# A perceiver block on one core: the first step's orders laid anew, and the gate's logits taken from transposed unnormalised tokens

## The chip, the core and the metric

One core of a Trainium2 chip runs the whole program. The metric is the device time in microseconds of one execution; lower is better. The core has five engines with queues of their own, each worked off in order: TensorE (PE; its weight loads are shown as PEld), VectorE (DVE), ScalarE (ACT), GpSimd (POOL) and SyncE (SP), which issues most DMA transfers. They wait for one another with semaphores only.

## What is computed

Three residual layers on 32 batches of 32 tokens of 512 channels, that is T = 1024 tokens: cross-attention to 257 context rows per batch with 16 heads, a mixing layer in the frequency domain, and a mixture of 8 experts of which each token takes the one with the largest gate logit.

```python
x = x + xattn(layernorm(x), ctx, ctx, mask)     # Q = ln(x) Wq.T + bq; softmax; weights @ V; @ Wo.T + bo
x = x + mix(layernorm(x))                       # sum over tokens of bind(k, v), unbound by each q (FFT)
l = layernorm(x)                                # (x - mean) / sqrt(var + eps)
logits = l @ Wg + bg                            # 512 x 8
one_hot = one_hot(argmax(logits), 8)
x = x + sum_e one_hot[:, e] * (gelu(l @ W1[e]) @ W2[e])
```

## The kernel before

Tokens lie in NT = 8 tiles of 128; HT = 4 of them are a half. KC = 4 chunks of 128 channels. Products are made in float16 with each operand split in a high half (`hi`, ScalarE, a rounded copy) and a low half (`lo`, VectorE, what the rounding left), so that one product is three passes: high x high, high x low, low x high (`hl_passes`). A layer norm takes `bn_stats` and `bn_aggr` on VectorE, the power −0.5 on GpSimd (`power`), and the normalisation `(x − mean) * rstd` on VectorE (`normalise`). `LN_GROUPS` lists the tiles of each norm: groups 0 and 1 are the halves for the cross-attention, 2 and 3 those for the mixing, 4 (tiles 0 to 3), 5 (4, 5) and 6 (6, 7) those for the experts.

The cross-attention runs in STEPS = 16 steps of two batches. Step 0 is laid out by hand (`first_step` on ScalarE and VectorE, a straight list on TensorE and GpSimd), steps 1 to 15 are a loop. In step 0 TensorE makes the keys of the first context (`first_keys`), its values (`first_values`), transposes of the normalised tokens in fp32 (`transpose_tokens`), eight query products (`queries`, one per half of the tokens and chunk), the keys and values of the 257th context row (the two products that count `last_ps`), and the scores of both batches. ScalarE moves each result out (`query`, `tokens_hi`), GpSimd rounds queries (`query_hi`), VectorE takes the low halves (`query_lo`, `tokens_lo`). SyncE stores the last row's values to DRAM and loads them again re-laid (semaphore `vlast_stored`); VectorE's `scores` may only write after that store, since both use the same memory. GpSimd spreads the queries over the heads (`queries_of`, counts `q_ready`). After the softmax the probabilities' high and low halves are transposed by DMA (`p_transposed`: one transfer per batch, once `p_lo` is done), and the attention of step 0 stands behind the keys of step 1 on TensorE.

The third layer norm and the gate overlap the end of the mixing layer. `spectra` are 24 products of 512 columns, in two banks; ScalarE moves each out. VectorE's `bind` and `unbind` form the spectrum of the result, `back` on TensorE is the inverse transform in fp32 (16 products of 256 columns for a half of the tiles), and `x2` on VectorE adds it to the tokens. Then per tile: normalise, high half (`l2_split`, ScalarE), low half (`l2_lo`: GpSimd for tiles 0 to 5, VectorE for 6 and 7), eight float16 transposes (`gate_transpose`), one copy out (`gate_transpose_out`) and twelve products of 8 columns with `wg` (`gate`). From the logits VectorE makes the one-hot of the largest; TensorE counts ranks with matmuls of a triangle and of ones; VectorE writes the slot matrices (`slots`); TensorE gathers the first expert's tokens with them (`first_gather`, 64 products of 160 columns), and VectorE moves them out (`first_gathered`), upon which `expert(0)` starts. Expert weights come in 8 pieces of 1 MB; `piece_hi` (ScalarE) and `piece_lo` (VectorE) halve each of them, and SyncE loads the next pieces behind counts of `e_lo`. Its queue at this point is: the pieces 0 to 6 of expert 0, the two halves of the normalised tokens (`l2_stored`, each behind the `l2_lo` of its tiles), piece 7, the residual tokens (2 MB), and the pieces of expert 1.

TensorE's list around the routing:

```python
for t in range(HT, NT): back(t, 0)
for t in range(HT, NT): back(t, 1).then_inc(s["irfft_ps"], 1)
for t in range(HT): gate_transpose(t)
for t in range(HT): gate(t)
gate_transpose(HT); gate_transpose(HT + 1); gate_transpose(HT + 2)
gate(HT); gate_transpose(HT + 3)
for t in range(HT + 1, NT): last = gate(t)
```

## Time and profile before

| | us |
|---|---|
| median of 3 runs | 810.28 |
| the other two runs | 810.23, 2812.57 |
| the profiled execution | 810.39 |
| its span on the core | 808.3 |
| mean granted TensorE clock over the span | 0.982 of 2.4 GHz |

The run of 2812.57 is a single disturbed one; the other two and the profiled execution agree within 0.2 us. The page counts from the span's first instruction; 2.1 us lie around it. A row of the timeline has the start, the length from its first start to its last end, the engine, the line and what is done by how many instructions, and in brackets the idle time before it and who ended it.

### The profile page before, as it was taken

Reading aid. Unit: us, or ns where it says so; the run is one execution under the profiler, and the core shown is the slowest. Engines: PE = TensorE matmul, PEld = TensorE weight load, DVE = VectorE, ACT = ScalarE, POOL = GpSimd, SP = SyncE. Lnnn points to the kernel's source line nnn. Section 1 sums busy time; section 2 is a strip of 40 time slices with the busy share of each in tenths; the row PEclk is TensorE's granted clock in tenths of the full one; section 3 lists DMA queues with packets and bytes.
Section 4 is the critical chain, followed back from the end, with each engine's and each line's share of the span. In section 5 each row is a group of like instructions: output and inputs, shape, how many; then the busy total and the mean of one; then the engine's idle time right before and its main releaser. Section 6 shows DMA issues by size and latency. Waiting matters only on the chain.

```text
span 808.3 us, 22182 instructions
## 1 busy us (share of the span) xinstructions
PE 773.9 (96%) x8851; PEld 461.5 (57%) x8851; DVE 625.0 (77%) x990; ACT 470.1 (58%) x847; POOL 241.2 (30%) x413
## 2 busy tenths in 40 slices
PE   8987999999999999999999999996899999999995
PEld 3444455554455554455556545555868867876783
DVE  5877888888887887777768668787797879788860
ACT  4634656647665656665647034246478668766950
POOL 0143344332454333443322200004053323242220
PEclk9999999999999999999999999997799999999998
DMA  8335253444233443234423511102899998988500
GB/s 305 140 116 108 51 146 80 107 107 81 66 84 90 107 107 75 86 86 127 122 55 56 210 50 56 53 0 92 278 353 411 410 378 324 369 330 327 223 31 15
DMA packets 94901, 125.56 MB, mean 155 GB/s; under 512 B 76352, under 2 KB 79168, under 8 KB 83956
## 3 DMA queue, kind: packets, MB, share of 16 engines
q1 hardware_dynamic: 92260, 117.65, 45.6%
q0 software_dynamic: 2576, 7.02, 2.4%
q8 instruction: 44, 0.72, 0.3%
q14 instruction: 21, 0.17, 0.1%
HBM read 100.47 MB, written 6.88 MB: 133 GB/s over the span
## 4 chain that ended last, share of the span: by engine, by line
PE 79%; DVE 12%; ACT 3%; DMA 3%; issue 1%; POOL 1%; SPq 0%; POOLq 0%; DVEq 0%; ACTq 0%
PE bank L1470 58%; PE bank L1841 10%; PE bank L1632 4%; DVE arena L931 3%; PE bank L1813 3%; PE bank L1598 3%; ACT arena L696 2%; DMA arena<-arena 2%; DVE arena L987 2%; DVE arena L993 1%; ACT arena L663 1%; DMA arena<-in_wv_t 1%; DVE arena L1009 1%; PE bank L1800 1%; DVE arena L963 1%
## 5 line engine op out<-in xcount | busy, mean ns | idle before, releaser
L1470 PE MATMUL bank<-arena 128*128 128x160 f16 (+6 forms) x3992 | 572.7, 304 | 9.9 <-DVE arena L931 3.8
L1470 PEld LDWEIGHTS bank<-arena 128*128 128x128 f16 (+1 forms) x3992 | 327.8, 100 | 243.1 <-issue 12.0
L663 ACT ACTIVATE arena<-arena 128x256 f16<-128x256 f32 (+5 forms) x302 | 254.0, 889 | 23.6 <-PE bank L1813 10.1
L931 DVE SCALAR_TENSOR_TENSOR arena<-arena 128x2048 f16<-128x2048 f32 (+4 forms) x102 | 201.1, 1991 | 32.0 <-ACT arena L663 31.5
L663 ACT ACTIVATE arena<-bank 128x512 f16<-128x512 f32 (+1 forms) x175 | 100.1, 585 | 149.5 <-PE bank L1470 112.3
L931 DVE SCALAR_TENSOR_TENSOR arena<-bank,arena 128x512 f16<-128x512 f32 (+1 forms) x174 | 116.7, 682 | 48.3 <-ACT arena L663 44.7
L1841 PE MATMUL bank<-arena 128*128 128x512 f16 x384 | 86.6, 379 | 0.0
L696 ACT ACTIVATE arena<-arena 128x257 f32<-128x257 f32 x128 | 63.5, 498 | 26.3 <-DVE arena L995 26.3
L532 POOL TENSOR_TENSOR arena<-arena 32x1024 f16<-32x1024 f32 (+1 forms) x16 | 34.1, 2133 | 143.7 <-PE bank L1632 143.5
L1841 PEld LDWEIGHTS bank<-arena 128*128 128x128 f16 x384 | 36.2, 98 | 41.1
L549 POOL COPY arena<-arena 32x256 f16 (+1 forms) x128 | 50.3, 393 | 24.0 <-DVE arena L931 11.8
L987 DVE SCALAR_TENSOR_TENSOR arena<-bank,arena 128x257 f32<-128x257 f32 x128 | 53.5, 481 | 4.3 <-PE bank L1598 4.3
L1009 DVE SCALAR_TENSOR_TENSOR arena<-arena 128x256 f16<-128x256 f32 x128 | 54.0, 483 | 0.0
L890 ACT ACTIVATE arena<-bank 128x320 f32<-128x320 f32 x64 | 27.0, 422 | 45.7 <-PE bank L1470 45.7
L619 POOL DMA_INDIRECT arena<-l_dram,arena x14 | 28.0, 1999 | 82.9 <-PE bank L1800 53.5
L1406 DVE SCALAR_TENSOR_TENSOR arena<-arena 128x320 f16<-128x320 f32 x64 | 29.8, 487 | 25.1 <-ACT arena L663 25.1
L858 ACT ACTIVATE arena<-bank,arena 128x512 f32<-128x512 f32 x24 | 16.5, 687 | 46.6 <-PE bank L1470 46.2
L610 POOL DMA_INDIRECT out<-arena x16 | 16.1, 1006 | 86.4 <-DVE arena L1398 65.9
L993 DVE TENSOR_REDUCE arena<-arena 128x4 f32<-128x1028 f32 x32 | 39.2, 1224 | 1.1
L518 POOL TENSOR_TENSOR arena<-arena 128x256 f16<-128x256 f32 (+1 forms) x64 | 39.3, 635 | 1.2
L468 POOL TENSOR_TENSOR arena<-arena 128x4 f32<-128x4 f32 (+1 forms) x7 | 6.5, 926 | 110.9 <-DVE arena L939 110.8
L1632 PE MATMUL bank<-arena 128*64 128x64 f16 x1792 | 33.0, 198 | 4.4 <-DMA arena<-arena 4.3
(110 smaller groups left out, 467.1 us busy)
## 6 DMA issues: line engine op xcount, KB each, us to landing
arena<-in_w SPq DMA_DIRECT2D x64, 1024.0 KB, 7.6
arena<-in_ctx_t SPq DMA_DIRECT2D x15, 1024.0 KB, 5.5
arena<-in_awt SPq DMA_DIRECT2D x3, 1024.0 KB, 7.1
l_dram<-arena SPq DMA_DIRECT2D x4, 512.0 KB, 3.8
x_dram<-arena SPq DMA_DIRECT2D x1, 2048.0 KB, 14.4
arena<-in_wk_t SPq DMA_DIRECT2D x4, 256.0 KB, 4.9
arena<-in_ctx_t SPq DMA_DIRECT2D x4, 256.0 KB, 5.7
arena<-in_wv_t SPq DMA_DIRECT2D x1, 1024.0 KB, 8.7
```

The source lines that it names most:

```text
L518: g.tensor_tensor(q_bd[n][:, :, b, :].rearrange("p c (r q) -> p c r q", r=2), qT[n][:, :, bass.ds(st * (PB * S) + b * S, S)].unsqueeze(2) ...
L532: g.tensor_tensor(vl_cur[0:LAST_ROWS], vl_all[:, bass.ds(m, 1), :].broadcast_to((LAST_ROWS, PAIRS, P)), diag.unsqueeze(2).broadcast_to((LA ...
L549: g.tensor_copy(attT[n][own, :, bass.ds(m * (PB * S), PB * S)] .rearrange("p c (b q) -> p c b q", b=PB), att_st[n][own, :, :, r % 2, :]).t ...
L663: return a.activation(dst, src, ACT.Copy, scale=scale)
L696: a.activation(sm[:, j, :], sm[:, j, :], ACT.Exp, bias=neg_max[:, j:j + 1], scale=ISD / (SX * SK), accum_out=score_sums[:, j:j + 1]).then_ ...
L931: return v.scalar_tensor_tensor(dst, src, scale, h, ALU.mult, ALU.subtract)
L987: v.scalar_tensor_tensor(sm[:, j, :], bank[:, 0:L], bank[:, L:L + 1], mask_bias, ALU.add, ALU.add).then_inc(s["s_free"], 1)
L993: v.reduce_max(row_max[:, js], sm[:, js, :], AX_X).then_inc(s["s_max"], 1)
L1009: v.scalar_tensor_tensor(p_hl[1][b][:, j - b * KC, :], sm[:, j, 0:LM], recip[:, j:j + 1], p_hl[0][b][:, j - b * KC, :], ALU.mult, ALU.subtract
L1470: last = m.matmul(out_ap, w, x, start=(n == 0), stop=(n == len(pairs) - 1))
L1632: last = m.matmul(BG[own, cols], w[:, own], x[:, at * HALF:(at + 1) * HALF], start=(n == 0), stop=(n == len(pairs) - 1))
L1841: last = m.matmul(BC[:], hid_hl[z][:, f, 0:P], w[u][:, g, :], start=(f == 0 and u + z == 0), stop=(f == FC - 1 and z == 1))
```

## The change

In the first step: the normalised tokens of the cross-attention are made by ScalarE (`normal`: an Identity activation with scale rstd and bias shift = −mean * rstd) where VectorE made them; GpSimd multiplies the shift behind each power. The first values' passes run by halves and not by chunks. TensorE makes the second half's transposes and query 3 before the last row's products, which change banks, and one query fewer (5 and not 6) before the scores. ScalarE's and VectorE's lists follow; the last row's bias (`bv_hi`, `bv_lo`) goes behind query 4.

Around the gate: TensorE transposes the tokens as they are, unnormalised and in fp32 (four transposes a tile), and multiplies them with `wg` in fp32 (four products a tile). With s = the column sums of `wg`, made by matmuls of ones, the logits are rstd * (x Wg) + shift * s + bg, put together on VectorE in four operations. The normalised tokens for the experts are made by ScalarE inside `l2_split`, all low halves by GpSimd. `piece_lo(0, 3)` moves from the place before the logits to the place of `normalise(4)`, `piece_lo(0, 5)` behind the first gather's copies and the slots of all experts. TensorE makes 4 and 5 products of 512 columns whose result is not used (`keep_clock`), before the wait for the one-hot and before the first gather, which now also waits for the last low half.

```diff
-        Q_BANKS = (BA, BB, BA, BB, BA, BB, BA, BG)
+        Q_BANKS = (BA, BD, BB, BA, BB, BA, BB, BG)
@@ GpSimd, first step
-            power(0)
-            power(1)
+            def power_and_shift(n):
+                power(n)
+                ts = slice(LN_GROUPS[n][0], LN_GROUPS[n][-1] + 1)
+                pool.wait_ge(s["ln_rstd"], n + 1)
+                g.tensor_tensor(shift[:, ts], minus_mean[:, ts], rstd[:, ts], ALU.mult).then_inc(s["ln_shift"], 1)
...
-            for n in range(KC):
+            power_and_shift(0)
+            query_hi(0)
+            power_and_shift(1)
+            for n in range(1, KC):
                 query_hi(n)
@@ GpSimd, gate (l2_shift(n): as power_and_shift, counting l2_shift)
-            for n in range(2, 5):
-                power(n)
+            power(2)
+            power(3)
+            l2_shift(4)
             pool.wait_ge(s["unbound"], 4)
             for t in LN_GROUPS[4]:
                 l2_lo(t)
-            power(5)
+            l2_shift(5)
             l2_lo(LN_GROUPS[5][0])
+            l2_shift(6)
             l2_lo(LN_GROUPS[5][1])
-            power(6)
+            for t in LN_GROUPS[6]:
+                l2_lo(t)
@@ ScalarE, first step
+            def normal(n):
+                act.wait_ge(s["ln_shift"], n + 1)
+                for t in LN_GROUPS[n]:
+                    a.activation(xhat0[:, t, :], x_tok[:, t, :], ACT.Identity, bias=shift[:, t:t + 1],
+                                 scale=rstd[:, t:t + 1]).then_inc(s["ln_out"], 1)
...
                 v_first(0)
+                normal(0)
                 v_first(1)
...
                 query(1)
+                normal(1)
                 query(2)
+                tokens_hi(lnT_tile, 0, 1)
+                query(3)
                 act.wait_ge(s["last_ps"], 1)
@@ ScalarE, gate
             def l2_split(t):
-                if t in LN_GROUPS[5]:
-                    act.wait_ge(s["l2_normal"], t - HT + 1)
-                else:
-                    act.wait_ge(s["ln_out"], 2 * NT + (t + 1 if t < HT else t - 1))
+                act.wait_ge(s["l2_shift"], 1 + (t >= HT) + (t >= HT + 2))
+                a.activation(l2_f[:, t, :], x_tok[:, t, :], ACT.Identity, bias=shift[:, t:t + 1],
+                             scale=rstd[:, t:t + 1]).then_inc(s["l2_normal"], 1)
+                act.wait_ge(s["l2_normal"], t + 1)
                 hi(l2_tile(0, t), l2_f[:, t, :], 1.0).then_inc(s["l2_hi"], 1)
...
             gate_transpose_out(HT)
+            gate_transpose_out(HT + 1)
+            l2_split(HT)
+            gate_transpose_out(HT + 2)
+            l2_split(HT + 1)
+            gate_transpose_out(HT + 3)
             l2_split(HT + 2)
             l2_split(HT + 3)
@@ VectorE, first step
                 v_first(0)
-                normalise(0, xhat0)
                 v_first(1)
...
-                normalise(1, xhat0)
...
+                query_lo(1)
+                tokens_lo(lnT_tile, 0, range(HT, HT + 2))
+                query_lo(2)
+                tokens_lo(lnT_tile, 0, range(HT + 2, NT))
+                query_lo(3)
                 dve.wait_ge(s["last_hi"], 1)
@@ VectorE, gate
-            normalise(4, l2_f)
+            piece_lo(0, 3)
             bind(1, 1)
...
-            normalise(6, l2_f)
-            dve.wait_ge(s["l2_lo"], HT + 2)
-            for t in LN_GROUPS[6]:
-                l2_lo(t)
-            piece_lo(0, 3)
...
+            dve.wait_ge(s["gate_sums_ps"], 1)
+            v.tensor_scalar(gate_sums, BD[:, 0:E], 1.0 / (SX * SG), None, ALU.mult).then_inc(s["gate_sums_done"], 1)
+            dve.wait_ge(s["gate_sums_done"], 1)
+            dve.wait_ge(s["l2_shift"], 3)
+            v.tensor_tensor(gate_base, by_tile(gate_sums), by_expert(shift), ALU.mult).then_inc(s["chain_dve"], 1)
             dve.wait_ge(s["logits_ps"], 1)
...
                     piece_lo(0, 4)
-                    first_gathered(0)
-                    first_gathered(1)
+                    for c in range(KC):
+                        first_gathered(c)
+                    slots(own_rank)
                     piece_lo(0, 5)
-                    first_gathered(2)
-                    first_gathered(3)
-                    slots(own_rank)
@@ TensorE, first step
             queries(range(2, 3))
+            transpose_tokens(0, xhat0, 1)
+            queries(range(3, KC))
...
-            transpose_tokens(0, xhat0, 1)
-            queries(range(3, KC))
             pe.wait_ge(s["tr_free"], NT)
-            queries(range(KC, KC + 2))
+            queries(range(KC, KC + 1))
@@ TensorE, gate
             def gate_transpose(t):
-                pe.wait_ge(s["l2_lo"], t + 1)
+                pe.wait_ge(s["x2_done"], t + 1)
...
+                for c in range(KC):
+                    last = m.transpose((BG, BH)[t % 2][:, c * P:(c + 1) * P], x_tok[:, t, c * P:(c + 1) * P], ident)
...
+                return product(BC[:, t * E:(t + 1) * E], [(x2T[:, t, c, :], wg_stage[:, c, :]) for c in range(KC)])
+            def keep_clock(times):
+                for _ in range(times):
+                    m.matmul(BF[:].rearrange("p (c x) -> p c x", c=KC), ones16, ones16.unsqueeze(1).broadcast_to((P, KC, P)),
+                             start=True, stop=True)
...
             for t in range(HT, NT):
                 back(t, 0)
+            for t in range(HT):
+                gate_transpose(t)
+            gate_column_sums()
             for t in range(HT, NT):
                 back(t, 1).then_inc(s["irfft_ps"], 1)
```

## Rows read from the trace of the kernel before

**Rows 1.** The page: busy us, share of the span and instructions of each engine.
```profile
PE 773.9 (96%) x8851; PEld 461.5 (57%) x8851; DVE 625.0 (77%) x990; ACT 470.1 (58%) x847; POOL 241.2 (30%) x413
```

**Rows 2.** Waits of TensorE, whole span: us in total, times, longest us.
```profile
PE bank L1632 <- DMA arena<-arena: 4.3, 2, 4.2
```

**Rows 3.** Timeline of TensorE, around the gate.
```profile
541.97 3.69 PE L1470 MATMUL bank<-arena 128*128 128x256 f32 x16 [0.29 <-DVE arena L1269]
...
553.12 1.05 PE L1470 MATMUL bank<-arena 128*128 128x8 f16 x36
...
569.43 7.33 PE L1470 MATMUL bank<-arena 128*128 128x160 f16 x64 [1.95 <-DVE arena L1362]
577.46 14.39 PE L1470 MATMUL bank<-arena 128*128 128x160 f16 x232 [0.70 <-DVE arena L1369]
```

**Rows 4.** Chain that ended last, first 100 us: start us, us, what.
```profile
71.32 5.54 DMA arena<-arena
...
76.90 1.71 PE bank L1632 x56
78.61 1.43 PE bank L1598 x23
```

**Rows 5.** Table by microsecond: busy us (instructions) per engine, granted clock, DMA share, GB/s.
```profile
77.00:78.00 1.00, 1.00 (x42) 1.00 (x44) 0.00 (x0) 0.00 (x0) 0.00 (x0) 0.50 0.99 418
...
554.00:555.00 1.00, 0.63 (x19) 0.45 (x15) 0.97 (x3) 1.00 (x2) 0.00 (x0) 0.83 0.86 286
...
575.00:576.00 1.00, 1.00 (x16) 1.00 (x15) 1.00 (x1) 0.00 (x0) 0.00 (x0) 0.93 1.01 352
```

**Rows 6.** Timeline of TensorE, first step.
```profile
25.33 1.94 PE L1483 MATMUL bank<-arena 128*128 128x128 f32 x16
...
33.19 3.62 PE L1542 MATMUL bank<-arena 128*128 128x512 f16 x16
...
47.90 5.35 PE L1470 MATMUL bank<-arena 128*128 128x512 f16 x24 [1.52 <-DVE arena L931]
53.19 0.85 PE L1598 MATMUL bank<-arena 64*64 64x258 f16 x24
```

**Rows 7.** Timeline of VectorE, first step.
```profile
24.36 1.92 DVE L946 TENSOR_SCALAR arena<-arena 128x512 f32<-128x512 f32 x4 [0.37 <-POOL arena L468]
...
53.85 1.68 DVE L987 SCALAR_TENSOR_TENSOR arena<-bank,arena 128x257 f32<-128x257 f32 x4 [4.30 <-PE bank L1598]
```

**Rows 8.** Timeline of ScalarE, around the last spectra and the gate.
```profile
531.94 1.90 ACT L663 ACTIVATE arena<-arena 128x2048 f16<-128x2048 f32 x1
...
554.24 0.82 ACT L873 ACTIVATE arena<-arena 128x512 f32<-128x512 f32 x1
555.09 0.63 ACT L663 ACTIVATE arena<-arena 128x512 f16<-128x512 f32 x1
```

**Rows 9.** Timelines of GpSimd, then of SyncE's queue, first step.
```profile
47.87 2.15 POOL L518 TENSOR_TENSOR arena<-arena 128x256 f16<-128x256 f16 x2
...
51.25 0.21 POOL L522 COPY arena<-arena 128x8 f16<-128x8 f16 x1
...
60.80 0.20 POOL L498 TENSOR_TENSOR arena<-arena 128x4 f32<-128x4 f32 x1
...
44.68 3.57 SPq L359 DMA_DIRECT2D vlast_dram<-arena  x8
49.30 1.38 SPq L363 DMA_DIRECT2D arena<-vlast_dram  x4
```

**Rows 10.** Timeline of VectorE, around the gate.
```profile
530.82 1.91 DVE L946 TENSOR_SCALAR arena<-arena 128x512 f32<-128x512 f32 x4 [1.02 <-POOL arena L468]
...
547.56 0.69 DVE L1279 TENSOR_TENSOR arena<-arena,bank 128x512 f32<-128x512 f32 x1 [1.35 <-PE bank L1470]
```

**Rows 11.** Groups by line and form, 541.9 to 568: count, busy us, mean ns, idle before.
```profile
L1470 PEld LDWEIGHTS bank<-arena 128*128 128x128 f32 x32 | 5.9, 190 | 2.5 <-issue 1.8
```

**Rows 12.** The line that loads expert pieces, 545 to 600.
```profile
DMA to landing us min/median/max: 5.0/9.2/17.7
```

155 lines of the change are left out of this document (80 added, 75 removed).

## The prediction

> **What bounds the kernel now.** I read the page's busy shares first: TensorE is busy 96% of the span [rows 1], so whatever TensorE starts earlier counts, and nothing else does. The waits of TensorE [rows 2] then say where the missing 4% lies. Between the two stretches that the change touches it hardly waits. The longest, 4.2 us, is for a DMA transpose in the first 80 us; around the routing it waits up to 2 us at a time, as for the slot matrices at 569.43 [rows 3]. The chain of work [rows 4] shows what the first of these hangs on: VectorE's last low halves of the first probabilities, the DMA transpose of 5.54 us, then TensorE at 76.90. The tables by microsecond [rows 5] add the clock: it is at half (1.2 GHz of 2.4) from about 76.9 to 80.2, after TensorE had stood still since 72.7, and again from 554.8 to 575.1, after a stretch of short transposes and 8-column products. So two dates matter, since TensorE sets the end behind both: attention(1) of step 1 at 76.90, and expert 0 at 577.46 [rows 3].
>
> **Part 1, the first step.** TensorE, before, had these marks: transposes at 25.33, queries 0 and 1 completed by 36.8, queries 4 and 5 until 53.2, scores at 53.19, the last query until 60.2 [rows 6].
> Removed from VectorE: the two normalisations, 1.92 and 2.2 us, and 0.37 us of waiting for the power [rows 7]. Added to ScalarE: eight Identity activations. The row for that form and size is 0.82 us alone, a Copy of the size 0.63 [rows 8]; back to back they overlap a little, so I take 0.73 each, 2.95 us for four (bounds 2.5 and 3.3). GpSimd adds a multiply of 128x4 behind each power: 0.20 us by its own row of that size [rows 9] and about 0.2 of semaphore.
> Walking the queues with these: the first power ends at 24.33, the shift at 24.8, ScalarE normalises until 27.7 where VectorE was done at 26.3. v_first(1) is queued behind it on ScalarE, so VectorE gets it at 28.3 in place of 26.19, and its queue (low half of wq 2.3, tokens 2.4) ends at 33.8 in place of about 31.7. TensorE: last transpose 28.25, values 3 until 30.95, then 16 completing products at 33.85, done at 37.4. It is 0.6 us late there. The value product's new order of passes saves its 0.5 us wait before 17.49, but the transposes wait for the power anyway.
> Then query 2 (2.7 us) until 40.1. token_stats(1) ends at 38.3 on VectorE, the power and shift at 39.8, ScalarE normalises until 42.75, transposes until 43.2 (about 1.1 us of pacing), query 3 until 45.9, the two last-key products (2.2) until 48.1, query 4 until 50.85. One query fewer stands ahead of the scores. The two bias rows leave ScalarE's queue ahead of query 0, where nothing waits for them.
> What lets the scores start? Three things that fall together. (a) q_ready: GpSimd needed 47.87 to 51.46, 3.6 us, behind last_lo 2 [rows 9]; last_lo 2 moves to 48.75, so 52.4. (b) SyncE's eight stores and their landing took 44.68 to 49.30, 4.6 us, behind last_lo 1 [rows 9], now at 48.2: 52.85, before which VectorE may not write a score. (c) TensorE at 50.85 waits 1.5 us for (a). So VectorE's scores start at 52.95 against 53.85 [rows 7].
> From there I follow the second batch: scores(0,1) on TensorE at 56.0, VectorE reaches them at 58.2 (after the bias row, 1.2), maxima done 61.65 against 63.4, exp until 63.9, reciprocals at 64.85 against 65.95, p_hi until 66.6, k_lo(0) 67.8, p_lo until 70.2 against 71.3. The transpose lands 5.54 us later, at 75.8: **1.1 us** earlier. TensorE starts step 1 at 62.3 (60.48 before), has its keys done at 73.0 and the first attention at 74.05, so it waits 1.75 us in place of 4.2. The tables of rows 5 show half clock only after the 4.2 us, none after the 1.5 to 1.6 us waits before 32.32 and 47.90. The slow stretch cost 1.71 − 1.07 on the attention and 1.43 − 0.85 on the scores, **1.2 us** [rows 4, 6]. Sum of part 1: 2.3 us gained. Bounds: 0 (the three falling together a little worse, and the clock lost) and 3.5 (faster Identities, and the waits for q_ready and the store shorter by as much).
>
> **Part 2, the gate.** First a loss. piece_lo(0, 3) (2.29) moves from 562.44, where it stood ahead of the logits, to where normalise(4) stood, at 529.9 on VectorE. Its high half is ready on ScalarE only at 533.84 [rows 8, 10]. So VectorE waits, ends at 536.15, and bind(1,1) begins there in place of 532.65: 3.5 late. Queued behind it are both unbinds, for which TensorE's inverse products wait. ScalarE now also makes the four Identities of group 4 between spectra 20 and 21, about 1.42 us per pair with its high half [rows 8], 5.7 in all where only the four high halves stood; spectrum 23 waits for the bank until 541.05 and ends at 543.7, inside VectorE's delay. The inverse products of parity 0 begin at 545.35 against 541.97 and end at 549.05; the unbind ends at 549.0, so the 0.70 us wait before parity 1 is gone. Four transposes (0.121 each by the fp32 row [rows 6]), paced by copies out of 0.65, and the 8 column-sum products stand next, until 551.6; then parity 1 for tiles 4 to 7. x2 follows its first product by 1.2 [rows 3, 10], at 552.8 against 547.56. Four x2 at 2.1 and two sets of statistics at 0.55, now with no wait for the power, end at 562.5 against 558.35: 4.2 late.
> Then the gain. Before, from 558.35: power 0.7, normalise, high half, low half, transpose, copy 1.02, gate, logits at 565.25: 6.9 us. Now only a raw transpose, one copy and one product follow x2_done. But the gate's products are fp32. In this trace one fp32 product is two loads and two passes: 32 loads for 16 products. The f16 products of 8 columns run at 1.05/36 = 0.029 us each [rows 3]; the nearest fp32 stream with short moving side is the transposes, 0.121 each; the loads of the inverse products are 0.190 long [rows 11], beside 256 columns. A tile has 8 loads: 0.23, 0.97 or 1.52 us. I take 0.97, since the load of 128x128 in fp32 is the same as in the transposes.
> The Trainium skill ("TensorE: Matmul & The Clock Gate", section "Weight-path perf modes") says the fast weight load is off for fp32, which speaks against this part of the change; by its formula for a load (section "LDWEIGHTS (loading the stationary operand)": columns over 1.2 GHz) an estimate would be 0.85 a tile in place of my 0.97. The trace agrees as far as it shows f16 and fp32 streams 0.029 and 0.121 apart; nothing above rests on it.
> TensorE then: parity 1 until 555.3, gates 0 to 3 until 559.0, transposes 4, 5 until 560.0, gate 4, transpose 6, gate 5, transpose 7 until 563.15, gate 6 until 564.1. ScalarE has copies and splits in turn (0.65 and 1.42): its copy of tile 7 ends at 564.9, gate 7 at 565.95. The shift of group 6 is there at 564.5, behind l2_lo(4) on GpSimd, still ahead of the logits. Logits need four steps in place of one, three of 0.25 more, the argmax 1.3: one-hot at 568.05 against 566.77. Slot matrices 2.6 later, 570.7 against 569.4. The last l2_lo is on GpSimd at 568.9, so it hides.
> Now the gather. Before, 64 products took 7.33 us, nearly all at 1.2 GHz, and VectorE's piece_lo(0, 5) stood ahead of its last two copies: 577.46 [rows 3]. Now the nine 512-column products (0.43 each at half clock) fill TensorE from 565.95 to 567.65 and from 568.6 to 570.7, and the clock, surely low by 562 as it was from 554.8, should be back by about 571, as it was back 5.6 us after TensorE's work became dense at 569.43 [rows 3, 5]. 64 x 0.0675 = 4.3 at full clock, 0.3 for a slow start, 0.5 for the last copy: expert 0 begins at **575.8, 1.7 us** earlier.
>
> **Sum.** 810.39 of the profiled run (span 808.3 and 2.1 around it) − 2.3 − 1.7 = 806.4. The median of the runs shown is 810.28, 0.1 lower; I say 806.4.
>
> **Rivals.**
> (A) The forecast, both parts small gains, 804.5 to 808.5: 0.48.
> (B) More: the 8-column fp32 products stream like the f16 ones. Then gate 7 waits for ScalarE and x2 only, the one-hot comes at 566.0, the expert at 573.7: 804.3; with Identities at 0.63 in part 1 another 0.6, 803.7. For it: the array passes only 8 columns. Against: the fp32 transposes' row. 0.17.
> (C) The gate gives nothing: the clock stays at 1.2 GHz through the gather as before. 570.7 + 7.4 + 0.5 = 578.6, 1.1 late: 809.2; with part 1 halved, 810.3. For it: the long run of 8-column products from 555.3. Against: the filling products. 0.20.
> (D) Slower: expert 0's last piece. Its load stands in SyncE's queue behind the stores that wait for the last l2_lo, which moves from about 562.5 to 568.9; it is issued at 570.0 in place of 564.75, and the 2 MB store of x2 behind it. ScalarE needs it in the third step of expert 0, at about 582.6, and all of the expert queues behind. Loads of this line took 5.0 to 17.7 us to land [rows 12]. From 12.6 us on TensorE waits; at 17.7 it costs 5.1: 811.5. From 16.6 us on this alone decides the sign. Median 9.2 speaks against it. 0.08.
> (E) Slower through the loads at 0.190 a piece: 8 x 0.55 = 4.4 late, the clock not back in time, 3 more: 813. Zero is crossed at 0.18 a load. 0.07.
>
> **Numbers.** The range takes (A), (C), most of (B) and (D): 802.5 to 811.5. 2% is 16 us (faster than 794.1 or slower than 826.5), about what a measurement of this kernel can tell from no change; no case comes near either: same 0.98, faster 0.01, slower 0.01.
>
> **What would show it.** Part 1: TensorE's wait before the second attention about 1.8 us and granted clock 1.00 in 75 to 80; scores near 52.9 with GpSimd or the store as releaser. A wait still over 3 us there makes it wrong. Part 2: VectorE idle some 3.5 us before piece_lo near 530 to 536, TensorE idle twice between 539 and 545.4; fp32 loads of the gate at 0.12; the statistics 4 us later; 64 gather products in under 5 us. If VectorE does not idle there, part 2 gains up to 3 us more; if the gate's loads are over 0.15 or the gather takes 7 us, it loses.

## The result and the profile after

| | before | after |
|---|---|---|
| median, us | 810.84 | 814.12 |
| lowest and highest, us | 810.23, 2812.57 | 813.07, 817.08 |
| runs | 8 | 8 |
| span of the profiled execution, us | 808.3 | 811.7 |
| granted TensorE clock, mean | 0.982 | 0.984 |

The ratio after to before is 1.0044, 95% interval 1.0034 to 1.0054: 3.6 us slower (2.8 to 4.4), where 4 us less was forecast, and outside the range. By the bound of 2% it is no change, and eight runs of each settle the sign. The ratio is of undisturbed runs only and leaves the run of 2812.57 out.

TensorE is busier than before, and the end is later [rows 1]:

```profile
PE 784.1 (97%) x8804; PEld 467.5 (58%) x8804; DVE 617.7 (76%) x982; ACT 476.9 (59%) x861; POOL 243.3 (30%) x420
```

The first date, attention(1) of step 1, went from 76.90 to 78.21 [rows 4]. Timelines of TensorE, VectorE, ScalarE, GpSimd and SyncE's queue after, first step (start, length, engine, line, what, count, idle time before and its releaser):

```profile
26.46 2.39 PE L1513 MATMUL bank<-arena 128*128 128x128 f32 x16 [1.39 <-ACT arena L730]
...
34.20 3.63 PE L1577 MATMUL bank<-arena 128*128 128x512 f16 x16 [0.70 <-DVE arena L959]
...
42.31 2.78 PE L1513 MATMUL bank<-arena 128*128 128x128 f32 x16 [1.89 <-ACT arena L730]
...
53.31 0.85 PE L1635 MATMUL bank<-arena 64*64 64x258 f16 x24 [0.95 <-POOL arena L530]
...
78.21 1.38 PE L1669 MATMUL bank<-arena 128*64 128x64 f16 x56 [3.91 <-DMA arena<-arena]
...
55.12 1.68 DVE L1024 SCALAR_TENSOR_TENSOR arena<-bank,arena 128x257 f32<-128x257 f32 x4 [4.64 <-DMA vlast_dram<-arena]
...
25.22 2.93 ACT L730 ACTIVATE arena<-arena 128x512 f32<-128x512 f32 x4 [2.31 <-POOL arena L482]
...
41.45 2.93 ACT L730 ACTIVATE arena<-arena 128x512 f32<-128x512 f32 x4 [2.89 <-POOL arena L482]
...
38.64 1.38 POOL L471 TENSOR_TENSOR arena<-arena 128x4 f32<-128x4 f32 x1 [1.09 <-DVE arena L1002]
40.10 1.31 POOL L482 TENSOR_TENSOR arena<-arena 128x4 f32<-128x4 f32 x1
...
50.04 3.57 SPq L362 DMA_DIRECT2D vlast_dram<-arena  x8
```

TensorE now waits for ScalarE's Identities (L730) before both sets of transposes. The four scores of VectorE start at 55.12 behind the landed store of the last row's values, where they started at 53.85 [rows 7]; everything to the DMA transpose hangs on them, and TensorE waits 3.91 us as before [rows 2].

The second date, expert 0, went from 577.46 to 581.54 [rows 3]. Timelines of TensorE and VectorE after, around the gate:

```profile
542.14 2.76 PE L1500 MATMUL bank<-arena 128*128 128x512 f16 x12 [1.64 <-ACT arena L889]
546.82 3.69 PE L1500 MATMUL bank<-arena 128*128 128x256 f32 x16 [1.91 <-DVE arena L1305]
...
552.73 7.37 PE L1500 MATMUL bank<-arena 128*128 128x8 f16 x56
559.96 1.92 PE L1760 MATMUL bank<-arena 128*128 128x128 f32 x8
561.78 1.87 PE L1500 MATMUL bank<-arena 128*128 128x8 f32 x8
563.50 1.09 PE L1760 MATMUL bank<-arena 128*128 128x128 f32 x4
564.39 1.71 PE L1500 MATMUL bank<-arena 128*128 128x8 f32 x8
565.96 1.09 PE L1760 MATMUL bank<-arena 128*128 128x128 f32 x4
566.84 3.42 PE L1500 MATMUL bank<-arena 128*128 128x8 f32 x16
...
575.71 5.25 PE L1500 MATMUL bank<-arena 128*128 128x160 f16 x64
581.54 14.39 PE L1500 MATMUL bank<-arena 128*128 128x160 f16 x232 [0.59 <-DVE arena L1401]
...
535.28 2.29 DVE L959 SCALAR_TENSOR_TENSOR arena<-arena 128x2048 f16<-128x2048 f32 x1 [4.01 <-ACT arena L684]
...
570.30 0.23 DVE L1361 SCALAR_TENSOR_TENSOR arena<-bank,arena 128x64 f32<-128x64 f32 x1 [3.93 <-PE bank L1500]
```

VectorE waits 4.01 us before the low half of piece 3, and TensorE twice before the inverse products, as forecast. But from 559.96 to 570.12 TensorE works through the fp32 transposes and products of tiles 4 to 7 without a gap, and VectorE waits 3.93 us for the last of them. The table by microsecond (busy us and instructions of PE, PEld, DVE, ACT, POOL; granted clock; DMA share; GB/s):

```profile
79.00:80.00 1.00, 1.00 (x34) 0.87 (x34) 0.00 (x0) 0.32 (x1) 0.23 (x1) 0.50 0.06 25
...
559.00:560.00 1.00, 1.00 (x11) 1.00 (x12) 0.97 (x4) 0.00 (x0) 0.83 (x2) 1.00 0.05 16
560.00:561.00 1.00, 1.00 (x6) 1.00 (x7) 0.97 (x3) 0.00 (x0) 0.06 (x1) 0.50 0.00 0
...
577.00:578.00 1.00, 1.00 (x16) 1.00 (x15) 1.00 (x1) 0.00 (x0) 0.00 (x0) 0.96 1.12 336
```

At 560.0 the clock falls to half, and the table counts 6 fp32 instructions in a microsecond where it counted 11 (it counts one in each microsecond that it touches). It had fallen at 554.7 before [rows 5] and was back at 575.1; now it is back at 577.1. The first row belongs to the first date: the attention of step 1 still runs into half clock.

### The profile page after: what moved, and what is told of

It reads as the page before. It is cut to its first block, busy times and chain, and to the rows that moved or that the text cites. A ratio compares the mean times of both kernels' runs of the same rounds, so it can differ in the third digit from the quotient of the medians.

```text
span 811.7 us, 22103 instructions
## 1 busy us (share of the span) xinstructions
PE 784.1 (97%) x8804; PEld 467.5 (58%) x8804; DVE 617.7 (76%) x982; ACT 476.9 (59%) x861; POOL 243.3 (30%) x420
## 4 chain that ended last, share of the span: by engine, by line
PE 83%; DVE 8%; ACT 4%; DMA 3%; issue 1%; SPq 1%; POOL 1%; POOLq 0%; DVEq 0%; ACTq 0%
PE bank L1500 61%; PE bank L1888 10%; PE bank L1669 4%; PE bank L1860 3%; PE bank L1635 3%; DVE arena L959 2%; DMA arena<-arena 1%; ACT arena L684 1%; DVE arena L1024 1%; DMA arena<-in_wv_t 1%; ACT arena L717 1%; DVE arena L1030 1%; DVE arena L1046 1%; PE bank L1847 1%; PE bank L1760 1%
## 5 line engine op out<-in xcount | busy, mean ns | idle before, releaser
L1500 PE MATMUL bank<-arena 128*128 128x160 f16 (+8 forms) x3920 | 567.5, 305 | 6.5 <-DVE arena L1305 1.9
L1500 PEld LDWEIGHTS bank<-arena 128*128 128x128 f16 (+3 forms) x3920 | 328.9, 102 | 234.4 <-issue 12.6
L684 ACT ACTIVATE arena<-bank 128x512 f16<-128x512 f32 x175 | 100.0, 584 | 144.9 <-PE bank L1500 111.3
L959 DVE SCALAR_TENSOR_TENSOR arena<-bank,arena 128x512 f16<-128x512 f32 x174 | 117.0, 682 | 55.9 <-ACT arena L684 52.3
L1669 PEld LDWEIGHTS bank<-arena 128*64 128x64 f16 x1792 | 30.4, 113 | 11.1 <-issue 6.4
```

Source lines behind the costliest of these rows:

```text
L684: return a.activation(dst, src, ACT.Copy, scale=scale)
L959: return v.scalar_tensor_tensor(dst, src, scale, h, ALU.mult, ALU.subtract)
L1500: last = m.matmul(out_ap, w, x, start=(n == 0), stop=(n == len(pairs) - 1))
L1669: last = m.matmul(BG[own, cols], w[:, own], x[:, at * HALF:(at + 1) * HALF], start=(n == 0), stop=(n == len(pairs) - 1))
```

## The experiments

The kernels ran on several chips, on which the kernel before took 811 or 816 us; every ratio is against runs of the kernel before on the same chip, with a 95% interval. Dates of two traces can't be laid side by side to a tenth, since the first loads land up to a microsecond apart; where it matters they are counted from a mark of their own trace. One kernel, `before_again`, is the kernel before itself, once more for its trace (span 807.9, attention(1) at 77.31, expert 0 at 577.49).

> The kernel before itself, for a profile on the same chip as its neighbours. Second attention of step 1 near 77, expert 0 near 577.5 to 578.5; the stretch from expert 0 to the end shows whether this chip spends longer there than the first one's 230.8 us.

### Each part alone

`step1_only` has the first step's part, `gate_only` the gate's with its unused products; each is the diff above, halved.

> Only the first step's new orders; the gate is that of before. Theory: the two parts add up, and this one alone delays the second attention of step 1 from 76.9 to about 78.2, with VectorE's first scores waiting for the store of the last row's values near 55.1; so 1.3 us over before, about 812.1. Rival: the first step's loss in the changed kernel is only its later first loads (0.5 us) and the rest is made up by the end; then 810.8 to 811.3.

> Only the gate's part; the first step is that of before. Theory: expert 0 begins 2.7 us later than in before (about 580.1), since the gate's fp32 loads of tiles 4 to 7 run at half clock at 0.21 each; about 813.5. Rival: the gate's delay came from the shifted start of the clock's fall and is gone with the old first step; then 811 or less, with expert 0 before 578.

Measured: `step1_only` 1.0001 (0.9988 to 1.0014), `gate_only` 1.0041 (1.0022 to 1.0059). The loss is the gate's. The first step's part, forecast at −2.3 us, gives nothing, and the 1.3 us that `step1_only` was expected to lose are not there either. The trace of `gate_only` has the same gate as after: tile gates of 1.87 and 1.71 us, the clock at half from 559.4 to 576.5, expert 0 at 581.30.

### The gate: what the fp32 loads cost

`gate_f16`: the transposed tokens go out as float16 and are multiplied with the high half of the weights; the low halves of both are left out, so the logits are less exact. One scale factor on VectorE is changed to match.

```diff
-        x2T = ea.take([NT, KC, P], F32)
+        x2T = ea.take([NT, KC, P], F16)
...
-                return product(BC[:, t * E:(t + 1) * E], [(x2T[:, t, c, :], wg_stage[:, c, :]) for c in range(KC)])
+                return product(BC[:, t * E:(t + 1) * E], [(x2T[:, t, c, :], wg_hl[0][:, c, :]) for c in range(KC)])
```

> The gate part alone, with the transposed tokens moved out as float16 and multiplied with the high half of the gate's weights in float16: 4 products of 8 columns a tile and no fp32 load among them (the low halves of both operands are left out, so some tokens near a tie go to another expert). Theory (the fp32 loads of the gate's products on TensorE carry the loss): a tile's gate takes about 0.2 us instead of 0.95 and 1.75; TensorE then waits for the residual additions and ScalarE's copies; the last gate ends near 564.5 where it was 570.2, the one-hot comes near 567.5, and expert 0 begins 4 to 6 us earlier than with fp32, near 576: ratio to before 0.997 (0.995 to 0.999). Rival (VectorE's and ScalarE's order carries it, the products are beside the path): expert 0 stays within 1 us of 581.3 and the ratio near 1.004.

Measured: 0.9984 (0.9974 to 0.9995), by the ratios 4.6 us below `gate_only` and 3.5 below its repetition `gate_fill`, both on other chips. Timeline of TensorE in `gate_f16`:

```profile
559.29 0.66 PE L1729 MATMUL bank<-arena 128*128 128x128 f32 x4 [1.92 <-DVE arena L1295]
559.78 0.24 PE L1476 MATMUL bank<-arena 128*128 128x8 f16 x4
561.39 1.12 PE L1729 MATMUL bank<-arena 128*128 128x128 f32 x4 [1.36 <-DVE arena L1295]
562.30 0.29 PE L1476 MATMUL bank<-arena 128*128 128x8 f16 x4
```

A tile's gate takes 0.24 us, TensorE waits for the residual additions again, and expert 0 stands 27.07 us behind the gate's first transposes (549.18), against 31.20 in `gate_only`. So the fp32 products carry the loss; with cheap ones the gate's part is a small gain (1.3 us).

`gate_clock` keeps them in fp32 and keeps TensorE dense: 18 unused products of 512 columns stand between the tiles of `gate_only` (`dense(n)` makes n of them; the lines here make 14).

```diff
             for t in range(HT):
                 gate(t)
+                if t == 0:
+                    pe.wait_ge(s["x2_done"], HT + 1)
+                dense(3)
             gate_transpose(HT)
             gate_transpose(HT + 1)
+            dense(2)
             gate(HT)
...
```

> The gate's part alone with 18 more unused 512-column products between the gate's tiles (3 behind each of tiles 0 to 3, 2 at three places later), 3.9 us of TensorE at full clock. Theory: what I sized wrong is the fp32 loads at half clock, 0.214 each against 0.108; with the clock held, a gate tile takes 0.87 us and a transposed tile 0.49 throughout, the logits are ready about 1.4 us earlier than in the gate's part alone (568.8 for 570.2) although 3.9 us of work were added, and the gather runs at full clock in 4.4 us: expert 0 near 579, 2 us before the gate's part alone. Rival: the loads of tiles 4 to 7 are slow for another reason (VectorE or ScalarE reading the same memory); then they stay near 0.2 with the clock at 1.00, and the time is 3 to 4 us over the gate's part alone.

Measured: 1.0045 (1.0031 to 1.0059). Its timeline of TensorE, and a row of its table by microsecond:

```profile
547.34 5.38 PE L1476 MATMUL bank<-arena 128*128 128x256 f32 x16 [1.91 <-DVE arena L1281]
...
566.76 0.63 PE L1729 MATMUL bank<-arena 128*128 128x128 f32 x4
...
567.66 0.95 PE L1476 MATMUL bank<-arena 128*128 128x8 f32 x8
...
577.38 5.13 PE L1476 MATMUL bank<-arena 128*128 128x160 f16 x64
...
548.00:549.00 1.00, 1.00 (x4) 0.82 (x3) 1.00 (x2) 0.00 (x0) 0.00 (x0) 0.50 0.00 0
```

At a granted clock of 1.00, from 551.2 to 575.1, a tile's gate takes 0.95 us, tiles 4 to 7 included, and at 0.50 in `gate_only` 1.71: the loads follow the clock, 0.119 and 0.214 us each. This refutes the rival that the loads of the last tiles are slow for another reason. Counted from the gate's first transposes, expert 0 stands 30.55 us behind and not 31.20 as in `gate_only`: 3.9 us of products were put in and 0.65 gained. The clock fell at 575.1 after all, once TensorE had waited 2.75 us for the one-hot, so that the gather took 5.13 us and not the 4.4 expected. The ratio shows no gain.

This trace has a second stretch of half clock, from 547.8 to 551.2, behind a wait of 1.91 us that `gate_only` has too, there with a clock of 1.00 behind it. The inverse products of parity 0 took 5.38 us for 3.69, and 1.7 us were lost ahead of the gate. So the dates of this trace can't be laid beside those of `gate_only` from any earlier mark, and that the products put in are what held the clock afterwards is not shown: the clock had come back at 551.2, just before.

### The gate: the unused products

`gate_nofill`, and on another chip side by side `gate_fill` (`gate_only` again) and `gate_idle` (`gate_nofill` again):

```diff
             pe.wait_ge(s["x2_done"], NT)
-            keep_clock(WAIT_FILLERS[0])
             pe.wait_ge(s["onehot_done"], 1)
...
-                keep_clock(WAIT_FILLERS[1])
                 pe.wait_ge(s["perm_done"], 2)
```

> The gate part alone without its nine unused products. Theory (they bring the clock back before the gather): TensorE stands still from 570.2 to 573 and from 573.9 to 575.8, the granted clock stays at half through most of the gather, which takes about 7.3 us instead of 4.9, and expert 0 begins 2.4 us later: ratio to before 1.007 against 1.004 with them. Rival (the clock comes back by itself with the gate's short products): the gather stays near 5 us, ratio 1.004.

> The same kernel as gate_only, on one chip with gate_idle, to measure what the nine unused products are worth. Theory (in the profiles they save 1.7 us between the first transposes and expert 0, since the gather takes 4.9 and not 7.0 us): ratio to before 1.004, and 0.2% below gate_idle. Rival (the saving is lost again behind expert 0): the two equal.

> The same kernel as gate_nofill, on one chip with gate_fill. Theory: gather 7.0 us at half clock, expert 0 31.2 + 1.7 us behind the first transposes, ratio to before 1.006. Rival: 1.004, as gate_fill.

Measured: 1.0044 (1.0031 to 1.0057) for the first, which alone said that the products are worth nothing; side by side 1.0027 (1.0014 to 1.0040) with and 1.0053 (1.0039 to 1.0067) without them: 2.1 us, the intervals just touching. In the traces of the pair the gather takes 5.53 us with and 6.36 without them, and expert 0 stands 31.20 and 32.86 us behind the gate's first transposes: 1.7 us. The traces of `gate_only` and `gate_nofill` say the same, 4.91 and 7.04 us, 31.20 and 32.88. The granted clock is back at 577 with them and at 579 without. The ratios of the two pairs, 0.0003 and 0.0026 apart, leave open how much of the 1.7 us reaches the end. `before_fill` puts the same nine products into the kernel before and moves `piece_lo(0, 5)` behind the copies of the gather:

> The kernel before with two small things of the change and nothing else: the 4 and 5 unused products in TensorE's waits, and piece_lo(0, 5) behind the first gather's copies. Theory: the gather's clock is worth most of the gate's part; TensorE is dense from 565.2 instead of from 569.4, the clock is back by 572, the gather takes some 5 us in place of 7.3 and VectorE's last copy follows at once: expert 0 near 575.3, 2.2 us earlier, ratio 0.9973. Rival: the loads of expert 1's pieces, which follow e_lo, take it back in the expert stage: ratio 0.999 to 1.000 with expert 0 2 us earlier.

Measured: 0.9962 (0.9948 to 0.9977), 3.1 us gained with none of the rest of the change. It is two edits, and they were not run apart. Timeline of TensorE in `before_fill`:

```profile
566.63 1.87 PE L1736 MATMUL bank<-arena 128*128 128x512 f16 x4
...
568.89 2.29 PE L1736 MATMUL bank<-arena 128*128 128x512 f16 x5
570.99 4.75 PE L1468 MATMUL bank<-arena 128*128 128x160 f16 x64
576.33 1.83 PE L1468 MATMUL bank<-arena 128*128 128x160 f16 x24 [0.59 <-DVE arena L1369]
```

The gather that took 7.33 us [rows 3], and 6.13 in `before_again` on the same chip, takes 4.75, and the wait for its copies out is 0.59 us and not 0.70 and 1.37. Counted from the gate's first transposes, expert 0 stands 24.88 us behind and not 27.58 and 27.05.

### The gate: the order

`piece3_back` moves only `piece_lo(0, 3)` of the kernel after, behind the last statistics.

> The changed kernel, but with VectorE's piece_lo(0, 3) behind the last x2 statistics in place of ahead of bind(1,1). Theory: TensorE is what sets the gate's end (it works without a pause from 550.3 to 570.1), so it gains what the wait for the unbind took, 1.9 us: parity 0 begins right behind spectrum 23, the ratio to the changed kernel is 0.998, about 812.2. Rival: VectorE and x2 set the end; then the whole 3.5 us of VectorE's delay come back, 810.6. Third: nothing, since the clock falls so much earlier that the gates take it back, 814.

Measured: 1.0031 (1.0018 to 1.0044), and the sibling below, with the low half in its place, 1.0040. The two gains that were expected, 1.9 or 3.5 us, did not come. TensorE still waits 1.64 us for ScalarE, and 1.13 for 1.91 us for VectorE. The logits were about 1 us earlier, but the gather took 6.14 us, since the clock came back only at 577.9: expert 0 at 581.45. Most of the microsecond gained ahead of the gather is given back in it.

`gate_woven` (from `gate_only`) moves three things: ScalarE's splits of tiles 0 to 3 behind the spectra, `piece_lo(0, 3)` behind the last statistics, and TensorE's first four gates each behind an inverse product.

```diff
-                if n == 20:
-                    for t in range(HT):
-                        l2_split(t)
...
+            for t in range(HT):
+                l2_split(t)
...
             for t in range(HT, NT):
                 back(t, 1).then_inc(s["irfft_ps"], 1)
-            for t in range(HT):
-                gate(t)
+                gate(t - HT)
```

> The gate's part alone, with three orders changed: the high halves of tiles 0 to 3 behind the spectra on ScalarE, piece_lo(0, 3) behind the last statistics on VectorE, and on TensorE the gates of tiles 0 to 3 each behind an inverse product of tiles 4 to 7. Theory: TensorE loses neither the 1.6 nor the 1.9 us waits at the spectra's end, the clock falls one stretch later, and part of the loads of tiles 4 to 7 run at full clock: logits near 563, expert 0 near 575 to 576, 2 us before the kernel before; ratio to it about 0.997. Rival: the waits only move to ScalarE's splits, GpSimd's low halves become the last (l2_lo of tile 7 sets the gather), and it ends level with before, ratio 1.000.

Measured: 0.9965 (0.9954 to 0.9977). Timelines of TensorE, VectorE and GpSimd in `gate_woven`:

```profile
560.51 0.96 PE L1475 MATMUL bank<-arena 128*128 128x8 f32 x8
...
568.25 0.24 PE L1778 MATMUL bank<-arena 128*128 128x64 f16 x1 [2.62 <-DVE arena L1353]
...
560.89 2.28 DVE L940 SCALAR_TENSOR_TENSOR arena<-arena 128x2048 f16<-128x2048 f32 x1
...
561.05 2.67 POOL L471 TENSOR_TENSOR arena<-arena 128x2 f32<-128x2 f32 x1 [0.17 <-DVE arena L950]
```

Three of the last four gates run before the clock falls (561.4), and the parity-1 additions start 3 us earlier. What is left in the way is the power of the last group: 2.67 us where the same form takes 0.70, because VectorE's low half started 0.16 us earlier and ran beside it. The Trainium skill ("SBUF — State Buffer", section "Who interferes with whom") says that a VectorE instruction with two inputs in SBUF contends with a GpSimd instruction that reads SBUF, that the port pair they share is an exclusive lock, and that the order of issue decides which of them blocks; this trace agrees: the power ends 0.55 us after the low half, at 563.72 against 563.17.

`woven_gap` puts that low half behind the last unbind, where VectorE stood still for 2.57 us.

> As gate_woven, and the low half of piece 3 stands behind the last unbind, where VectorE stood still for 2.57 us before the inverse products of parity 1. Theory (in gate_woven the one-hot was late because GpSimd's power took 2.67 us beside VectorE's low half, and the base of the logits another 1.09): power back at 0.7 us, logits wait for TensorE's last gate near 563.9, one-hot near 566.9 instead of 568.2, slot matrices 1.2 us earlier; the clock returns near 571.5 as before, so a part of the gather is at half clock, and 0.5 to 1.2 us are left: ratio to before 0.9955 (0.9948 to 0.9962). Rival (the date at which the clock returns decides the gather's end): ratio as gate_woven, 0.9965. Second rival: the low half ends after 550.7 and pushes all additions, then the gain is nothing too, with the additions late.

Measured: 0.9947 (0.9934 to 0.9961), 4.3 us faster than before; its interval overlaps that of `gate_woven`, so that the step from one to the other rests on the traces. Timeline of GpSimd, then of TensorE, in `woven_gap`:

```profile
560.55 0.70 POOL L471 TENSOR_TENSOR arena<-arena 128x2 f32<-128x2 f32 x1 [0.17 <-DVE arena L950]
...
566.54 0.24 PE L1778 MATMUL bank<-arena 128*128 128x64 f16 x1 [1.42 <-DVE arena L1353]
...
569.15 5.48 PE L1475 MATMUL bank<-arena 128*128 128x160 f16 x64
575.22 3.01 PE L1475 MATMUL bank<-arena 128*128 128x160 f16 x41 [0.59 <-DVE arena L1376]
```

The power takes 0.70 us. Counted from the gate's first transposes the rank products, and so the one-hot, come 1.2 us earlier than in `gate_woven` (20.20 and 21.40 us), and 0.5 of that is paid in the gather, again through the clock (5.48 against 4.97 us): expert 0 stands 28.88 us behind the first transposes, and 29.56 in `gate_woven`.

### The first step

`last_early` (from the kernel after) makes the last row's products, and all that hangs on them, ahead of the second half's transposes.

> The changed kernel, but the last row's products stand ahead of the second half's transposes on TensorE (in its wait for the normalisation), and their halves early on ScalarE and VectorE. Theory: the first scores waited for the store of the last row's values, which now lands near 48; they start with TensorE or GpSimd's q_ready, by 52, and the second attention of step 1 begins by 76.5, 1.5 to 2 us earlier than in the changed kernel, and the clock stays at 1.00: about 811.5. Rival: ScalarE's slower normalisation is what delays the step; then the scores start no more than 0.5 us earlier and the time is that of the changed kernel, 814.

Measured: 1.0040 (1.0022 to 1.0058). The last row's store is issued at 43.76 and not 50.04, VectorE's scores start at 53.56 behind TensorE's, and attention(1) at 77.69, where `piece3_back` on the same chip has its scores at 55.47 and attention(1) at 78.52 (53.35 and 54.46 us behind the first power). So the store was the last of the three releasers. The total does not show the 1.1 us; its interval is wider than that.

`order_only` (from `step1_only`) puts both normalisations back on VectorE and leaves GpSimd's multiplies out; the orders stay.

```diff
-            power_and_shift(0)
+            power(0)
...
-                normal(0)
...
-                normal(1)
...
                 v_first(0)
+                normalise(0, xhat0)
                 v_first(1)
...
+                normalise(1, xhat0)
                 query_lo(1)
```

> The first step's part alone, but with both normalisations back on VectorE (where it made them before) and without GpSimd's multiplies of the shift: the new order of TensorE, ScalarE and VectorE remains. Theory (the part gains nothing since ScalarE's Identities and GpSimd's multiplies give back what the order gains): TensorE's transposes start near 25.3 instead of 26.55 and its wait before the second transposes falls from 1.89 to about 1; VectorE's waits of 4.08 and 2.77 us take the normalisations in; the last row's store, the scores and the second attention come 1 to 1.5 us earlier than in step1_only: 77.3 instead of 78.6, ratio to before 0.9985. Rival (the chain over the last row's products, their low halves, the store to DRAM and its landing decides, and the order put it late): scores wait for the landed store as in step1_only, second attention after 78, ratio 1.000.

Measured: 0.9980 (0.9971 to 0.9990). Timelines of TensorE and VectorE in `order_only`:

```profile
25.50 1.94 PE L1508 MATMUL bank<-arena 128*128 128x128 f32 x16 [1.04 <-DVE arena L963]
...
32.06 3.63 PE L1572 MATMUL bank<-arena 128*128 128x512 f16 x16 [0.31 <-DVE arena L948]
...
75.56 1.71 PE L1664 MATMUL bank<-arena 128*64 128x64 f16 x56 [4.01 <-DMA arena<-arena]
...
51.91 1.68 DVE L1011 SCALAR_TENSOR_TENSOR arena<-bank,arena 128x257 f32<-128x257 f32 x4 [4.18 <-DMA vlast_dram<-arena]
```

The expected wait of about 1 us was 1.74, but the marks are early all the same: in `step1_only` the completing query products stand at 34.46 and attention(1) at 78.60. Since loads land at different times on the two chips, the marks are counted from the first power on GpSimd: the completing products stand 8.45 us behind it here and 10.34 in `step1_only`, attention(1) 51.95 and 54.48, and 53.6 in both traces of the kernel before. So the new order gains 1.7 us and ScalarE's Identities cost 2.5, of which 1.9 are there at the first of the two marks. `order_mult` adds GpSimd's multiplies again, with nobody waiting for them:

> order_only with GpSimd's multiply of the shift kept behind each of the first two powers, and nobody waiting for its result: only GpSimd is later by it. Theory (ScalarE's Identities carry the loss of the first step's part: TensorE waits for them before both sets of transposes): the multiply moves the roundings of queries on GpSimd by 0.2 and 1.3 us, which the slack before query 4 takes; second attention within 0.5 us of order_only's 75.56, ratio to before 0.998. Rival (the multiply of 1.3 us beside VectorE carries it): the roundings of queries 1 and 2 come 1.5 us late, and with them VectorE's low halves, the last row's store and the second attention, near 77: ratio 1.000.

Measured: 0.9973 (0.9964 to 0.9983), attention(1) 52.09 us behind the first power. The second multiply takes 1.31 us there too and costs nothing. What costs are the Identities on ScalarE: the move of `v_first(1)` behind them, and TensorE's wait for ScalarE, which itself waits for the multiply.

### Both repaired parts

`both_best` is the kernel after with the edits of `order_only` and `woven_gap`.

> Both repaired parts together: order_only's first step with woven_gap's gate. Theory (the parts lie in separate stretches, and what either gains reaches the end): the gains add, 0.9980 x 0.9947 = 0.9927, 804.9 us where before has 810.83; second attention near 75.6 to 76.5, expert 0 near 573.5. Rival (they share something, as the date at which the clock returns before the gather, or the arrival of the expert's pieces): no more than woven_gap alone, 0.9947. From 0.994 upward the rival holds.

Measured: 0.9938 (0.9923 to 0.9953), the fastest kernel here, 5.1 us below before. The gains about add (product 0.9927); the rival's 0.9947 also lies inside the interval, so that nothing is shared is likely and not shown. In the profiled execution 1.6 us were lost in the first step, by this table by microsecond and the timeline of TensorE:

```profile
41.00:42.00 1.00, 0.90 (x6) 0.88 (x6) 1.00 (x4) 0.60 (x1) 0.00 (x0) 0.70 0.00 0
42.00:43.00 1.00, 1.00 (x7) 1.00 (x6) 1.00 (x2) 0.67 (x2) 0.00 (x0) 0.50 0.00 0
...
40.37 3.37 PE L1512 MATMUL bank<-arena 128*128 128x128 f32 x16 [1.74 <-DVE arena L973]
43.53 3.39 PE L1499 MATMUL bank<-arena 128*128 128x512 f16 x12
```

The clock was at half for 3.4 us, from 41.4 to 44.8, behind a wait of 1.74 us that `order_only` has too (1.74), with a clock of 1.00 behind it and 2.32 and 2.75 us for the same two rows. It is what `gate_clock` shows at 547.8. How often it happens was not measured.

## Why the prediction was wrong, point by point

**Part 1: −2.3 forecast; +1.3 in the profile, +0.7 counted from the first power, nothing in the ratio of the part alone.** Right up to query 2: ScalarE's queue was worked out to delay the completing products to 33.85, and they stood at 34.20. The step that failed is the one after it, "the power and shift at 39.8". They ended at 41.41, 1.38 and 1.31 us long beside VectorE's subtractions (its low halves among them), where the sum had taken the small multiply at its solitary row of 0.20 [rows 9]. The 1.6 us went through the Identities, query 3 and the last row's products into the store, and the store with its landing took 5.1 and not 4.6 us, so that VectorE's scores started 2.2 us after the forecast 52.95. Some 0.6 of all this is no loss: the first loads landed later in this execution (first power at 23.86; it ended at 24.33 before, so it began at 23.3). From there all steps are as forecast and 2 us late: `p_lo` done at 72.04 (70.2), the transpose landed at 78.2 (75.8), after 6.06 us and not 5.54. TensorE's keys were done at 73.2 (73.0). So the wait stayed, and with it the half clock, from 78.7 to 82.1. Even `order_only`, 2.4 us faster, waits 4.01, since TensorE's list moved forward with the scores. The term "clock not lost", 1.2 us, was wrong in every kernel whose first step differs here. Together the 3.6 us between forecast and profile are 0.6 of later loads, 1.0 of the shift, 0.8 mainly of the two landings, and the 1.2 of the clock.

**Part 2, the loss ahead of the gate: right.** VectorE's wait was forecast at 3.5 and measured 4.01, TensorE's two waits were there (1.64, 1.91), and parity 0 began at 546.82 for 545.35, of which 1.3 is part 1. `woven_gap` shows that none of it was needed.

**Part 2, the gate's products: the term that failed.** "I take 0.97 [a tile], since the load of 128x128 in fp32 is the same as in the transposes" was right for the form and wrong for the clock. The row of 0.121 [rows 6] is one at full clock; the same text puts the clock "surely low by 562" and still prices all eight tiles by it. Measured, a tile's gate is 0.9 us while the clock is up (tiles 0 to 3) and 1.71 to 1.87 at half, a tile's transposes 0.5 and 0.9. From the start of the transposes of tile 4 to the last product 6.95 us were forecast and 10.3 passed: 3.3 us. It also decided what lies beside what: the logits were to wait for ScalarE's last copy, and waited for TensorE. `gate_f16` takes that cost out and gets the forecast's sign, `gate_clock` shows the loads at 0.119 when the clock stays up. The forecast's rival (E) had the place and nearly the size, loads at 0.190 for 0.214 measured, but its reason was the 256 columns beside them [rows 11], and it had 0.07. The mean of 190 ns that it took is no pace: the loads of gates 0 to 3, at full clock, have 192 ns in the same column, and 33 of them cover 3.9 us, 0.12 each, so the records overlap. The forecast's own sign of a loss, loads over 0.15, did appear.

**The unused products: the mechanism right, the date late.** They shorten the gather (5.25 after, 7.33 before), and are worth 2.1 us in the pair. The clock was to be back at 571, and was back at 577.1, for the products stood 4.2 us later than forecast (570.12 for 565.95), and TensorE's fp32 work before them had not brought it back. No row shows the 0.0675 us a gather product that the sum takes at full clock; 232 products of the form took 14.39 us [rows 3], 0.062 each, so this term was not too small.

**The sum by its own terms.** Part 1 was off by 3.6 us. Part 2 gained −1.7 by forecast and lost 581.54 − 577.46 − 1.3 = 2.8: off by 4.5, of which 3.3 is the fp32 stream, 0.7 the slower one-hot chain (2.8 and not 2.1 us), 0.7 the gather and copies (5.83 for 5.1), −0.2 the rest. From expert 0 to the end 230.2 us passed for 230.8: −0.7. Together 7.4, and 806.4 + 7.4 = 813.8 = 811.7 + 2.1, where 2.1 is what lay around the span before; around this one lay 1.8, and the profiled execution took 813.5.

**The rivals.** (D) did not occur: piece 7 was issued at 572.65, later than feared, and TensorE ran 14.39 us into expert 0 without a wait. (B) is refuted by the 11 instructions a microsecond at full clock, where its 0.23 us a tile would give about 34. (C) is half of what happened: the gather was short, but the products ahead of it paid for the low clock.

## What to carry to other kernels

A duration of TensorE read in a trace has a clock with it. Before a row prices new work on TensorE, look at which level the clock stands where the work will be; short fp32 work took 1.8 times as long at half clock here. And a wait that the new work fills with its own instructions is not hidden for free: ask whether the stretch is still bound by another engine once each instruction costs double. A small instruction on GpSimd is priced beside what VectorE does at that moment and not by its solitary row, above all if an engine waits for it.

## What the runs showed of the hardware

- An fp32 load with its short pass follows TensorE's clock: 0.119 us at 1.00 and 0.214 at 0.50 (8 columns, 128x128 loaded). The Trainium skill ("TensorE: Matmul & The Clock Gate", section "LDWEIGHTS (loading the stationary operand)") gives a load as its columns over 1.2 GHz, an estimate of 0.107 for this one; the trace agrees to about a tenth at full clock, and not at half, where the measurement is twice that.
- The 8-column float16 products follow it far less: 0.029 us each at full clock [rows 3], and 0.035 at half, by this row of TensorE's timeline in the kernel before (granted clock 0.50):

```profile
563.41 0.83 PE L1470 MATMUL bank<-arena 128*128 128x8 f16 x24
```

- GpSimd's power of 128x2 took 0.70 us alone and 2.67 us beside a VectorE instruction that had started 0.16 us earlier; its multiply of 128x4 took 0.20, and 1.31 beside one that had started 1.03 us earlier (39.07 after).
- A TensorE that is busy almost without a pause can lose its clock. In the kernel after it works from 550.3 to 572.0 with one wait of 0.4 us, and the clock falls at 560.0, during fp32 work that began soon after 552.7 (inverse products, the gates of tiles 0 to 3, the first transpose of tile 4). In `gate_clock`, with products of 512 columns between the same tiles, it is at 1.00 from 551.2 to 575.1; but there it had been at half from 547.8 to 551.2, which no other trace of this gate has, so what made the difference is open.
- The same waits in front do not decide it alone. Behind TensorE's waits of 1.64 and 1.91 us the clock stays at 1.00 in `gate_only` and falls for 3.4 us in `gate_clock`; behind 1.74 us it stays in `order_only` and falls for 3.4 us in `both_best`. One profile of each kernel does not say how often.
- It comes back in the dense stretch before or inside the gather: at 577.1 after (unused products from 570.12 on), at 571.3 in `before_fill` (from 566.63 on), at 579.0 in `gate_idle` (gather from 575.30 on), and at 575.1 and 573.2 in the two traces of the kernel before (gather from 569.43 and 569.99 on). That is 3.2 to 7.0 us behind the start of the dense work, so an earlier start helped in these traces, but not microsecond by microsecond.
